# Depooled patches and input bias: from a GpSimd add to TensorE's accumulation

## The reference

```
xn  = layernorm(x)
h   = rmsnorm(xn, g_res) @ W_in.T + b_in          # per token
hp  = rmsnorm(ctx[..., :128], g_init)             # per patch, 64 patches in a sequence
s_p = a * s_(p-1) + u(hp_p)                       # a scan over the patches, written as a matrix "decay"
out = s[plug(token)] + h                          # each token takes the patch that its place points to
x   = x + tanh(g_xattn[1]) * out
x   = x + tanh(g_ffn[1]) * top2_moe(layernorm(x)) # 8 experts, expert biases
```

## Time and profile before

| | |
|---|---|
| median of 3 runs | 494.19 us (491.52 to 498.88) |
| span of the profiled execution, first to last instruction | 490.0 us; the page states no other time for it |
| mean granted TensorE clock | 0.972 |
| busy: PE, PEld, DVE, ACT, POOL | 91%, 71%, 75%, 57%, 65% |

### The profile page before, as it was taken

The page is one execution under the profiler, slowest core; times in us unless marked ns, Lnnn a source line. Parts: engine busy times, 40 slices in busy tenths (PEclk is TensorE's granted clock), DMA queues, the critical chain, the costliest instruction groups (busy, mean ns, idle before and its releaser), DMA issues. The chain is left out here.

```text
span 490.0 us, 20510 instructions
## 1 busy us (share of the span) xinstructions
PE 443.7 (91%) x6871; PEld 349.2 (71%) x6872; DVE 366.8 (75%) x1201; ACT 277.8 (57%) x775; POOL 319.4 (65%) x780
## 2 busy tenths in 40 slices
PE   5789999989999999997987999987997799899998
PEld 3456677756766666774666988864655799898997
DVE  3668999978898989944768666545766678788984
ACT  2468899877988888764234545434233434444431
POOL 3845765567777777767723666577825899898630
PEclk9889999998999999989999999998999699999999
DMA  7941231111111110100245776631000011111001
GB/s 232 413 152 41 48 36 27 26 31 40 28 32 33 30 36 22 37 20 18 76 131 158 228 227 216 222 121 37 18 5 13 16 46 33 46 37 37 23 23 33
DMA packets 37394, 37.38 MB, mean 76 GB/s; under 512 B 20440, under 2 KB 31504, under 8 KB 36816
## 3 DMA queue, kind: packets, MB, share of 16 engines
q0 software_dynamic: 7552, 20.20, 12.9%
q1 hardware_dynamic: 29200, 16.06, 11.9%
q10 hardware_dynamic: 576, 0.26, 0.2%
HBM read 24.82 MB, written 7.86 MB: 67 GB/s over the span
## 5 line engine op out<-in xcount | busy, mean ns | idle before, releaser
L979 DVE TENSOR_REDUCE negm<-PS 128x4 f16<-128x512 f32 x128 | 81.9, 681 | 0.4
L716 ACT ACTIVATE pexp<-PS 128x512 f32<-128x512 f32 x128 | 69.4, 595 | 6.4 <-PE PS L1383 5.8
L1725 PE MATMUL PS<-w,vp 128*128 128x128 f32 x512 | 63.3, 277 | 0.0
L1725 PEld LDWEIGHTS PS<-w,vp 128*128 128x128 f32 x512 | 60.6, 194 | 0.0
L1396 PEld LDWEIGHTS PS<-pexp,vp 128*32 128x32 f32 x2048 | 34.5, 113 | 26.4 <-issue 20.5
L1396 PE MATMUL PS<-pexp,vp 128*32 128x64 f32 x2048 | 50.3, 230 | 0.3
L1619 PE MATMUL PS<-xsT,wst 128*128 128x128 f32 x320 | 44.4, 282 | 3.0 <-DVE stack L1217 1.3
L1619 PEld LDWEIGHTS PS<-xsT,wst 128*128 128x128 f32 x320 | 38.8, 191 | 7.3 <-issue 5.0
L581 POOL DMA_INDIRECT sorted_x<-VALL,posu x32 | 33.3, 1040 | 13.4 <-issue 7.6
L611 POOL DMA_DIRECT2D wst<-in_rt_gate_up_dram x40 | 21.5, 538 | 29.2 <-PE PS L1619 19.9
L1310 DVE TENSOR_TENSOR vp<-PS,xnT 128x1024 f32<-128x1024 f32 x32 | 38.6, 1205 | 0.8 <-PE PS L1702 0.8
(11 more groups left out here) (246 smaller groups left out, 1254.5 us busy)
## 6 DMA issues: line engine op xcount, KB each, us to landing
wst<-in_rt_gate_up_dram POOLq DMA_DIRECT2D x40, 256.0 KB, 3.5
xs<-sorted_x SPq DMA_DIRECT2D x40, 64.0 KB, 2.8
sorted_y<-YS POOLq DMA_DIRECT2D x40, 64.0 KB, 3.0
out_dram<-X SPq DMA_DIRECT2D x32, 64.0 KB
X<-in_x_dram SPq DMA_DIRECT2D x1, 1536.0 KB, 8.2
CK<-in_ctx_k_dram SPq DMA_DIRECT2D x1, 1536.0 KB, 12.2
CV<-in_ctx_v_swapped_dram SPq DMA_DIRECT2D x1, 1536.0 KB, 16.6
rdn<-in_rt_down_dram POOLq DMA_DIRECT2D x1, 1024.0 KB, 10.6
```

The lines of the kernel that those rows point to most:

```text
L716: nc.scalar.activation(pexp[:, j, :], PS[:, 2 + j % 2, :], ACT.Exp).then_inc(S["exped"], 1)
L979: dve.tensor_reduce(negm[:, a.par, :, j], PS[:, j % 2, :].rearrange("p (g k) -> p g k", g=G), AX.X, ALU.max, negate=True).then_inc(S["maxe ...
L1725: nc.tensor.matmul(PS[:, 6 + y.par, 0:D], z[:, y.par, e, :], w1[:, e * D:e * D + D], start=(e == 0), stop=False)
```

## The change

`place_patches` and `put_down` are gone from the filling, with their semaphores, and so is POOL's add. `dp` is now written straight into `DP`, and `pick`, one compare of 128x256 for a chunk in place of two of 64x256, goes into the part of `CK` that has been used. In stage 5 each tile's mixing group in bank 1 gets three more matmuls: the bias as a product of ones with a bias split in three bf16 parts (it shares the tile of the expert bias, now twice as wide), and for each of the two sequences a 64x64 `pick` with the 64x128 of `DP`. The four loads of the bias to 128x512 become three of one row, and ACT's scaling of it goes; DVE scales and splits the wider bias tile.

```diff
-            def place_patches(c):
...
-                for q in range(CT):
-                    at = slice(q * P, q * P + P)
-                    last = nc.tensor.matmul(PS[:, 3, at], pick[:, l.par, at], dp[:, l.par, at], start=True, stop=True)
-                last.then_inc(S["c_placed"], 1)
...
-            def put_down(c):
-                dve.wait_ge(S["c_placed"], Tile(c).done())
-                dve.tensor_tensor(DP[:, c * CT * D:(c + 1) * CT * D], PS[:, 3, :], binB4[:], ALU.add)\
-                    .then_inc(S["c_put"], 1)
...
-                dve.tensor_tensor(dp[:, f.par, :], PS[:, 7, :], ginit4[:], ALU.mult).then_inc(S["c_dp_kept"], 1)
+                dve.tensor_tensor(DP[:, c * CT * D:(c + 1) * CT * D], PS[:, 7, :], ginit4[:], ALU.mult)\
+                    .then_inc(S["c_dp_kept"], 1)
...
+                dve.tensor_scalar(CK[:, c * CT * D:c * CT * D + CT * SEQ], PS[:, 2, 0:CT * SEQ], patch_no, None, ALU.is_equal)\
+                    .then_inc(S["c_picked"], 1)
...
-                if f:
-                    pool.wait_ge(S["l_hn_ready"], f.done())
-                    if f.slot == 0:
-                        pool.wait_ge(S["c_put"], Tile(f.quad).done())
-                    pool.tensor_tensor(X[:, f.cols(D)], X[:, f.cols(D)], DP[:, f.cols(D)], ALU.add)\
-                        .then_inc(S["l_added"], 1)
...
-                    nc.tensor.matmul(PS[:, 1, 0:D], hnT[:, s.par, :], winT[:], start=True, stop=True)\
-                        .then_inc(S["l_mixed"], 1)
+                    nc.tensor.matmul(PS[:, 1, 0:D], hnT[:, s.par, :], winT[:], start=True, stop=False)
+                    nc.tensor.matmul(PS[:, 1, 0:D], ones16[0:3 * 32, :], b1s[:, D:2 * D], start=False, stop=False)
+                    if s.slot == 0:
+                        pe.wait_ge(S["c_dp_kept"], Tile(s.quad).done())
+                        pe.wait_ge(S["c_picked"], Tile(s.quad).done())
+                    for q in range(PAIRS):
+                        rows = slice(SEQ * q, SEQ * q + SEQ)
+                        last = nc.tensor.matmul(PS[rows, 1, 0:D], pick(s.t)[rows, :], DP[rows, s.cols(D)],
+                                                start=False, stop=True)
+                    last.then_inc(S["l_mixed"], 1)
...
-            scaled_by_gate(*((ginit4[:], 1), (binB4[:], 1), (w1[:, 0:512], 3), (w1[:, 512:1024], 3))[s - 4])
+            scaled_by_gate(*((ginit4[:], 1), (w1[:, 0:512], 3), (w1[:, 512:1024], 3))[s - 4])
...
-                dve.tensor_scalar(b1[:], b1[:], tgate[0:3 * 32, 3:4], None, ALU.mult).then_inc(bias_ready, 1)
+                dve.tensor_scalar(b1[:, 0:D], b1[:, 0:D], tgate[0:3 * 32, 3:4], None, ALU.mult).then_inc(bias_ready, 1)
+                dve.tensor_scalar(b1[:, D:2 * D], b1[:, D:2 * D], tgate[0:3 * 32, 1:2], None, ALU.mult).then_inc(bias_ready, 1)
```

More of the change, by code:

```diff
@@ L270, in down_bank, with pick @@
             return 4 + c % 2 if c < EARLY else 6
-        pick = zeros[:, 0:2 * CT * P].rearrange("p (s t) -> p s t", s=2)
+        def pick(t):
+            at = t // CT * CT * D + t % CT * SEQ
+            return CK[:, at:at + SEQ]
         plug16 = sb("plug16", [SEQ, SEQ], F16)
@@ L386, in flamingo_gated_two_layers @@
         plug_step = sem("plug_step")
-        for n in "hp_ready depooled dp_kept plugged picked placed put".split():
+        for n in "hp_ready depooled dp_kept plugged picked".split():
             S["c_" + n] = sem("c_" + n)
-        for n in ("x2 stats moments vars roots means shifts hn_ready hnT_done hnT_kept added mixed x3 stats2 moments2 "
+        for n in ("x2 stats moments vars roots means shifts hn_ready hnT_done hnT_kept mixed x3 stats2 moments2 "
                   "normed xnT_done xnT_kept routed choice spread mask_turned mask_kept masked "
@@ L491, in _ @@
             quad_credit(pool, ("k_score", 2), ("k_summed", 3))
-            credit(pool, *((n, 1) for n in "l_x2 l_vars l_roots l_means l_shifts l_added".split()))
+            credit(pool, *((n, 1) for n in "l_x2 l_vars l_roots l_means l_shifts".split()))
             pool.memset(idle[:], 0.0).then_inc(idle_zero, 1)
@@ L505, in _ @@
             late_loads = ((shd, sh_down), (rdn, rt_down), (w1, expert_w), (winT, w_in), (gres, g_res),
-                          (rw1, router_w), (rb1, router_b), *((b1[32 * k:32 * k + E], expert_b) for k in range(3)),
+                          (rw1, router_w), (rb1, router_b), *((b1[32 * k:32 * k + E, 0:D], expert_b) for k in range(3)),
                           *((ginit4[:, q * D:q * D + D], g_init) for q in range(CT)),
-                          *((binB4[:, q * D:q * D + D], b_in) for q in range(CT)))
+                          *((b1[32 * k:32 * k + 1, D:2 * D], b_in[0:1, :]) for k in range(3)))
             def sum_onehots(e):
@@ L651, in last_step @@
             def last_step(stage):
-                x, v, f, a = (stage(i) for i in (0, 2, 4, 6))
+                x, v, a = (stage(i) for i in (0, 2, 6))
                 if x:
@@ L899, in _ @@
             credit(dve, ("h_acted", 2), ("h_added", 1), ("e_acted", 1), ("e_kept", 1),
-                   *((n, 1) for n in ("c_dp_kept c_picked c_put l_stats l_moments l_x3 l_stats2 l_moments2 "
+                   *((n, 1) for n in ("c_dp_kept c_picked l_stats l_moments l_x3 l_stats2 l_moments2 "
                                       "l_masked l_out_ready").split()), ("l_choice", 4))
@@ L1733, in last_step @@
                     pe.wait_ge(S["l_mask_kept"], y.done())
-                    nc.tensor.matmul(PS[:, 6 + y.par, 0:D], mask1T[:, y.par, :], b1s[:], start=False, stop=True)\
+                    nc.tensor.matmul(PS[:, 6 + y.par, 0:D], mask1T[:, y.par, :], b1s[:, 0:D], start=False, stop=True)\
                         .then_inc(S["l_summed"], 1)
```

43 lines of the change are left out of this document (17 added, 26 removed).

## The result

The changed kernel takes **497.49 us** (median of four executions, 496.92 to 501.31); the kernel before, on the same chip, 496.31 (491.52 to 498.88). The ratio is **1.014, interval 1.009 to 1.020**; it leaves executions at a lower clock out and can't be formed from these eight times alone, whose medians lie 0.2% apart and whose lowest lie 1.1% apart. The profiled execution took 496.92 us with a span of 494.7, against 490.0 before: +4.7, where the sum said +5.0. The rest of the 1.5 us is the step from span to median, taken at 4.2 us and now 2.8 (497.49 - 494.7).

The account below looks back on a forecast made before the run. POOL was taken to set the pace from step 12, PE close behind; filling -3.4, sorted experts' start +0.5 and steps 12 to 36 +7.9 gave +5.0 us, span 495.0, plus 4.2 to the median: 499 us, range 491.5 to 507.

Parts of the forecast that it names:

- the sum: Whole span: filling -3.4, sorted experts' start +0.5, steps 12 to 36 25x - 6.14; +5.0 us at x = 0.56.
- x: PE's new work per mixing tile: bias pass 0.06, quarter passes 0.21, change of shape 0.29; together 0.56 us.
- The pairs: In the mixing group, the two sequences' quarter-array fp32 passes run together two by two, 0.21 us instead of 0.43.
- change of shape: In each mixing group, PE's array going to 64x64 blocks and back, with uncovered weight loads: 0.29 us.
- Rivals 1 and 2: Mixing's quarter passes run singly (x = 0.78, +10.5 us, 15%) or three turns deep (x = 0.67, +7.7 us, 17%).
- rival 3: In mixing, the change of shape hides behind neighbouring passes: x = 0.27, PE's pace 3.3 us, -2.3 us in all; 10%.
- The filling: Without placing, steps 1 to 4 gain 3.4 us until POOL's power of context scales sets the time; steps 5 to 8 nothing.
- Rival 4: In the filling, ACT's chain yields when PE is lighter: all eight blocks gained, -8 instead of -3.4 us; 8%.
- the half clock behind the filling: After the filling, some 10 us at 1.2 GHz; three steps' mixing near 0.9 us each, covered by PE's 2.7 us idle.
- the sorted experts' start: Before the last part, DVE's extra scaling and wider bias split, where PE waits for DVE: +0.5 us, between 0 and 0.9.
- POOL's step of 3.0: In steady mixing steps, POOL's step falls from 3.43 to 3.0 us without its add, just below PE's.
- rival 5: In the steady stretch, POOL's add is no real load and the pace stays 3.43 us for other reasons; no own chance.

Follow-up runs that it names:

- mixing alone: Changed kernel without the bias pass, the quarter passes and the two waits ahead of them, so output lacks patches and bias; 487.41 us.
- one-half kernel: Changed kernel with the second sequence's two fp32 passes replaced by one 16-bit pass on constants, its patches missing; 497.66 us.
- full pick: Changed kernel with one block-diagonal 128x128 fp32 matmul in place of the two 64x64 ones, same result; 491.68 us, ratio 1.0015.
- clock-kept kernel: Kernel before with patch add on VectorE, gather behind POOL's first add, and passes of zeros in PE's idle places; 484.54 us, ratio 0.988.
- blocks alone: Changed kernel with 32 matmuls of the placing's shape put back on PE in the filling, result unused, without VectorE's copy; 497.02 us.
- gather-later kernel: Kernel before with the patch add moved to VectorE and POOL's gather issued behind its first add of the step; 487.03 us, ratio 0.985.

## Why the prediction was right, point by point

- **PE's added work.** x = 0.56 was forecast; the pace says 0.55, or 0.57 against mixing alone (3.576 - 3.008 over steps 30 to 36). The pairs hold: the timeline shows them, and the one-half kernel. Two terms were mis-sized against each other: the bias pass costs 0.11, not 0.06, and the change of shape 0.24, not 0.29. The full pick shows both. That their sum came out is in part luck. Rivals 1 and 2 (0.78, 0.67) and 3 (0.27) are out. 24 steps were to take 86.3 us and took 86.13.
- **The filling.** Forecast: 3.4 to 3.5 us until step 4, nothing in steps 5 to 8; measured 3.55 and nothing. The wait that I said comes up is the one that did: from the end of POOL's power to the down matmuls I had 2.77 us, and it is 347.58 - 344.85 = 2.73. Rival 4 (all 8 us) is out.
- What I gave as a second reason, "about four blocks of placing would be 4", was wrong, and the right size hid it. The kernel before, by kernels that hold or lose the clock, lost its 3.55 us so: 1.5 to the half clock in steps 1 and 2 (11.98 us to step 2 with 3.4 us at half clock, 10.48 with none in the clock-kept kernel); 0.8 to copies, compares and what goes with the blocks there (10.48 against 9.69; with blocks alone it is 9.68), split no further by any run; 1.0 to PE's blocks and 0.26 to the rest in steps 3 and 4 (9.97, with blocks alone 9.72, without 8.71). The changed kernel falls to half clock at the same place (3.4 us from 332.4) and pays nothing: the one-half kernel, at full clock there, needs 18.37 us to step 4 and this one 18.40. This holds for 3.4 us: mixing alone, without placing too, had 6.8 us at half clock from the same place and needed 11.12 us to step 2 in place of 9.69, and 19.84 to step 4. So the loss that I had as a bound can come, and the changed kernel's 3.4 us were too short for it.
- **Mis-sized: the half clock behind the filling.** "PE is idle for 2.7 us of them, so this is covered" failed: 2.22 us were lost, 1.7 beyond the 0.56. I had priced the added passes and a fall of another length, not one at another place. The mixing-alone kernel has none and needs 18.34 us there against 16.96, so 1.38 of the 2.22 are not theirs. What has moved is the place of the half clock. It came 2.6 us earlier (376.7 against 379.3), but the filling ended 4.7 us earlier: it starts 4.6 us behind step 8's down matmuls in the kernel before, 6.7 in the changed one and 7.2 in mixing alone. It then lies on nearly all of step 11's expert matmuls, which take 3.22 and 3.62 us in place of 2.76; from them to step 12's it is 4.94 us in mixing alone (390.58 - 385.65) in place of 3.83. The gather-later kernel, also with no added pass, lies between (5.7 behind, 17.41 us). The other 0.84 (19.18 - 18.34) are the added passes, where 0.56 was forecast. Two mixings ran at half clock, not three, and the one right ahead of step 11's expert matmuls takes 0.9 us longer than in mixing alone, as I had estimated. Against the same kernel at full clock it is 2.4 us in all. Why the clock falls later behind the filling no run shows.
- **Mis-sized: the sorted experts' start.** +0.5 was taken, and the stretch grew by 0.19.
- **Wrong but without effect: POOL's step of 3.0.** It is 3.31, as the gather's issue time comes out from behind the add; rival 5, that the add is no real load, is right for 0.32 of its 0.43 us. At PE's 3.59 this is covered; had x been small, as in rival 3, it would have set the pace.
- The **sum** came within 0.3 us of the span (+5.0 against +4.66), partly by luck: the 1.7 us missed behind the filling are nearly the 1.47 us by which the attention was shorter in the profiled execution. Without that the changed kernel stands 6.1 us, 1.25%, behind, and the ratio's interval (0.9 to 2.0%) holds that.

## What to carry to other kernels

Before taking an instruction off the engine that sets the pace, look at what stands behind it in that queue: an issue time that it hides comes out when it goes, and the place of the next transfer may be worth more than the instruction. Work moved to the runner-up engine is paid in full from the point where the two meet; here 0.12 us a step could be had that way (POOL's 3.43 to 3.31) and 0.55 was moved, while moving the same add to VectorE and the gather behind another add gained 1.5%. And a slow stretch that idle time covers is not covered for good: ask what it will lie on once the work ahead of it is shorter. Here the same 10.2 us at half clock came 2.2 to 2.6 us later behind the filling, on the expert matmuls, which cost 1.4 us without one added pass.

## What was not expected of the hardware

- An indirect gather on POOL has 0.48 us of issue ahead of it when it follows a short instruction, and 0.16 when it follows an add of 0.45 to 0.51 us. It moved with the order of the instructions in all twelve traces, a few single gathers apart, whatever set the pace.
- Two 64x64 fp32 matmuls on opposite corners of the array, written one after the other into one bank, run as two pairs with starts some 0.01 us apart; entering and leaving that shape costs 0.24 us, as much as the passes themselves (0.21).
- A 16-bit pass of 0.06 us between fp32 ones costs 0.11 us: the weight loads around it start that far apart.
- The same fall of the clock costs very different times. At the start of the filling, 3.4 us at 1.2 GHz cost 1.5 us in the kernel before and none in the changed one, but 6.8 us cost 1.4 us in the mixing-alone kernel. Between steps 4 and 6, where PE waits for ACT, 3.4 us cost 1.5 us in mixing alone and 1.7 in one half. Behind the filling, 10.2 us cost the changed kernel 2.4; in the kernels with the old mixing the distance there is 16.96 and 17.41 us with 10.2 us at half clock and 16.64 with 3.4.
